# Three edge sweeps of a graph network on one core: who fetches the last column of every second group

## What is computed

```python
# layer 1 (four heads); layer 0 is alike, with one head and no edge term
alpha = a_src[src_a] + a_dst[dst_a] + a_edge
alpha = jnp.where(alpha > 0, alpha, NEG_SLOPE * alpha)
amax = jax.ops.segment_max(alpha, dst_a, num_segments=n)
alpha = jnp.exp(alpha - amax[dst_a])
denom = jax.ops.segment_sum(alpha, dst_a, num_segments=n)
out = jax.ops.segment_sum(alpha[:, :, None] * h[src_a], dst_a, num_segments=n)  # alpha over denom
# layer 3 (relations)
h = jnp.einsum('nd,rdo->rno', x, W_rel)
msg = h[edge_type, src]
agg = jax.ops.segment_sum(msg, dst, num_segments=n)
```

## Time and profile before

| | |
|---|---|
| Median of 3 runs | 9807.24 us (9797.97 to 9817.08) |
| Span of the profiled execution | 9691.9 us |
| The profiled execution's own time | not given beside its span |
| Gathers of the first attention sweep, first to last start | 324.2 to 2511.9 us |
| Gathers of the second attention sweep | 2950.7 to 6034.3 us |
| Gathers of the relation sweep | 6526.4 to 9500.0 us |
| Busy | POOL 51%, DVE 35%, ACT 11%, PE 7% |

### The profile page before, as it was taken

How to read it: one execution, slowest core, us unless ns; L and a number is a source line. 1 busy time by engine, 2 the same in 40 slices (tenths; PEclk the granted TensorE clock), 3 DMA queues, 4 the chain that set the end, 5 groups by cost and what they waited for, 6 DMA issues and landing times.

```text
span 9691.9 us, 57509 instructions
## 1 busy us (share of the span) xinstructions
PE 645.5 (7%) x2460; PEld 429.5 (4%) x2460; DVE 3381.8 (35%) x6204; ACT 1028.8 (11%) x3093; POOL 4970.1 (51%) x5237
## 2 busy tenths in 40 slices
PE   1100000000140000000000000580000000000000
PEld 1000000000140000000000000240000000000000
DVE  6555555555563222222222222761111111111113
ACT  1222222222120000000000000460000000000000
POOL 5766666666457444444444444216444444444445
PEclk7555555555565555555555555795555555555555
DMA  4456666666433222222222222452222222222222
GB/s 158 145 178 199 194 186 196 192 193 202 155 108 94 67 72 70 69 73 69 73 70 72 70 71 69 164 200 71 64 67 66 68 68 68 65 70 68 68 68 97
DMA packets 344911, 1045.34 MB, mean 108 GB/s; under 512 B 111529, under 2 KB 139564, under 8 KB 306594
## 3 DMA queue, kind: packets, MB, share of 16 engines
q1 hardware_dynamic: 157746, 670.54, 19.3%
q0 software_dynamic: 172192, 365.19, 14.8%
q10 hardware_dynamic: 14544, 5.93, 0.3%
HBM read 527.27 MB, written 513.96 MB: 107 GB/s over the span
## 4 chain that ended last, share of the span: by engine, by line
SPq 36%; issue 31%; DVE 14%; another core or an unknown queue 8%; PE 3%; POOL 3%; ACT 3%; ACTq 1%; DMA 1%; DVEq 0%; POOLq 0%
SPq L250 21%; SPq L249 7%; SPq L247 7%; DVE ps L1256 2%; DVE ps L1281 2%; POOL node_sums L1387 1%; DVE edge_rows L1286 1%; ACT edge_rows L1220 1%; DVE edge_rows L1264 1%; PE ps L2028 1%; ACTq L250 1%; DVE edge_logit L1356 1%; DVE feat_prod L1343 1%; DVE fine L592 1%
## 5 line engine op out<-in xcount | busy, mean ns | idle before, releaser
L1158 POOL DMA_INDIRECT edge_rows<-table_b,src_i x1523 | 1440.8, 946 | 1642.7 <-DMA sums_b<-edge_rows 1161.0
L2113 POOL DMA_INDIRECT edge_rows<-table_rel,rel_row x1523 | 1440.7, 946 | 1641.1 <-DMA sums_rel<-edge_rows 1096.3
L1158 POOL DMA_INDIRECT edge_rows<-table_a,src_i x1568 | 1485.0, 947 | 702.8 <-issue 487.3
L2197 DVE TENSOR_TENSOR edge_rows<-edge_rows,ps 128x1024 f32<-128x1024 f32 x195 | 237.9, 1220 | 2301.3 <-DMA edge_rows<-table_rel 2220.7
L1286 DVE TENSOR_TENSOR edge_rows<-edge_rows,ps 128x1032 f32<-128x1032 f32 (+1 forms) x390 | 484.2, 1241 | 962.5 <-remote 726.8
L1350 DVE TENSOR_TENSOR edge_rows<-edge_rows,ps 128x2112 f32<-128x2112 f32 (+1 forms) x99 | 230.9, 2332 | 1010.1 <-ACT ps L1223 961.8
L1220 ACT ACTIVATE edge_rows<-edge_rows,weight_decay 128x129 f32<-128x129 f32 x1560 | 493.6, 392 | 211.5 <-issue 211.3
L1281 DVE TENSOR_TENSOR ps<-edge_rows,ps 128x1032 f32<-128x1032 f32 (+1 forms) x390 | 485.6, 1245 | 8.6 <-issue 1.9
L1316 DVE TENSOR_TENSOR z<-edge_rows,dst_logit 128x16 f32<-128x16 f32 (+2 forms) x198 | 40.1, 203 | 1194.2 <-DMA edge_rows<-table_b 1171.4
L1223 ACT ACTIVATE ps<-weight_decay 128x128 f32<-128x128 f32 (+1 forms) x99 | 27.7, 280 | 3036.5 <-DVE weight_decay L1337 1562.8
L2144 ACT ACTIVATE ps<-keep 128x16 f32<-128x16 f32 x98 | 19.6, 201 | 2985.8 <-issue 1534.7
(11 more groups left out here) (296 smaller groups left out, 3207.3 us busy)
## 6 DMA issues: line engine op xcount, KB each, us to landing
sums_a<-edge_rows SPq DMA_DIRECT2D x98, 2064.0 KB
sums_b<-edge_rows SPq DMA_DIRECT2D x98, 1120.0 KB, 4.2
edge_rows<-in_ea SPq DMA_DIRECT2D x98, 1024.0 KB
sums_rel<-edge_rows SPq DMA_DIRECT2D x98, 1024.0 KB, 3.9
table_rel<-rel SPq DMA_DIRECT2D x98, 512.0 KB
edge_rows<-table_b SPq DMA_DIRECT2D x2880, 0.5 KB
edge_rows<-table_b ACTq DMA_DIRECT2D x2880, 0.5 KB
edge_rows<-table_rel ACTq DMA_DIRECT2D x2880, 0.5 KB
```

Of the source, the lines that this page charges most:

```text
L1158: e.indirect_dma_start(out=rows[:, s, i, 0:L.W], out_offset=None, in_=L.table, in_offset=bass.IndirectOffsetOnAxis(ap=src[:, at:at + 1], a ...
L2113: e.indirect_dma_start(out=rows[:, s, i, :], out_offset=None, in_=table_rel, in_offset=bass.IndirectOffsetOnAxis(ap=rel_row[:, at:at + 1], ...
```

## The change

The class `Helped` becomes `Gathers`, which only counts what POOL's gathers add to the semaphores. In the second attention sweep and in the relation sweep POOL gathers all sixteen columns of all 98 groups, and SP and ACT fetch nothing. `helped_src`, `helped_rel`, the two transposes and five small DVE instructions that made them in the graph stage, the registers and the extra waits of DVE go. Slots, stores, waits before the gathers and all arithmetic of the sweeps stay. The core of the diff (left out are the declarations of the two tiles and of the registers):

```diff
@@ -208,52 +205,26 @@
 
-    LAST = GC - 1
-
-    def every(n, first):
-
-        return {g: h for h, g in enumerate(range(first, NG - 1, n))}
-
-    def helped_columns(ap, place):
-
-        at = [natural(g, LAST) for g in place]
-        return ap[:, at[0]:at[-1] + 1:at[1] - at[0]]
-
-    helped_b = every(2, 7)
-
-    class Helped:
-
-
-        def __init__(self, name, place, index, table, W, rows, NS, stored, summed):
-            self.place, self.index, self.table, self.W = place, index, table, W
-            self.rows, self.NS, self.stored, self.summed = rows, NS, stored, summed
-            self.by_pool = {g: 16 * sum(GC - (i in place) for i in range(g % NS, g + 1, NS)) for g in range(NG)}
-            self.by_pool[NG - 1] -= 16 * GK
+    class Gathers:
+
+
+        def __init__(self, NS):
+            self.NS = NS
             self.first_half = sem_of("edges_first_half", 16 * GK)
-            self.fetched = [sem(f"{name}_helped{i}") for i in range(3)] if place else []
-
-        def all_by_pool(self, slot):
-            return self.by_pool[max(g for g in range(NG) if g % self.NS == slot)]
-
-        def fetch(self, e, regs, g, p0, n):
-
-            if g not in self.place:
-                return
-            h, s = self.place[g], g % self.NS
-            e.wait_ge(*self.stored[s].at(16 * (g // self.NS)))
-            e.wait_ge(*self.summed.at(g - self.NS + 2))
-            for p in range(p0, p0 + n, len(regs)):
-                m = min(len(regs), p0 + n - p)
-                e.load(regs[0:m], self.index[h:h + 1, p:p + m])
-                for i in range(m):
-                    row = e.snap(regs[i])
-                    e.dma_start(self.rows[p + i:p + i + 1, s, LAST, 0:self.W], self.table[bass.ds(row, 1), :]
-                                ).then_inc(self.fetched[h % 3].sem, 16)
+            self.slot = [sem_of(f"edges_gathered{i}", self.total(max(g for g in range(NG) if g % NS == i)))
+                         for i in range(NS)]
+
+        def total(self, g):
+            return 16 * GC * (g // self.NS + 1) - (16 * GK if g == NG - 1 else 0)
+
+        def landed(self, g, i):
+            return self.first_half if g == NG - 1 and i < GK else self.slot[g % self.NS]
+
+        def wait_half(self, e):
+            e.wait_ge(*self.first_half.at(16 * GK))
 
         def wait(self, e, g):
-            if g in self.place:
-                h = self.place[g]
-                e.wait_ge(*self.fetched[h % 3].at(16 * P * (h // 3 + 1)))
+            e.wait_ge(*self.slot[g % self.NS].at(self.total(g)))
 
@@ -470,8 +441,6 @@
         hc = sb("head_count", [P, GK])
-        helped_f = sb("helped_f", [P, 2, P])
-        helped_floated, helped_turned = sem("helped_floated"), sem("helped_turned")
         weights = Weights(A, sb, io["a_w"], io["a_att_src"], io["a_att_dst"])
@@ -638,9 +607,6 @@
                 t = then(e.tensor_copy(tmp_e[:, :], src[:, :]))
-                then(e.memset(helped_f[:, :, :], 0.0))
-                e.wait_ge(*step.at(step.n))
-                e.tensor_copy(helped_f[:, 0, 0:len(helped_b)], helped_columns(tmp_e, helped_b)).then_inc(helped_floated.sem, 1)
                 e.wait_ge(*zero_stored.at(N_ZERO))
@@ -649,7 +615,6 @@
                 then(e.tensor_copy(rel_row[:, :], tmp_e[:, :]))
-                e.tensor_copy(helped_f[:, 1, 0:len(helped_b)], helped_columns(tmp_e, helped_b)).then_inc(helped_floated.sem, 1)
                 yield
@@ -733,9 +698,6 @@
             then(e.tensor_copy(sum_row[:, :], s2[:, :]))
-            e.wait_ge(*helped_turned.at(1))
-            then(e.tensor_copy(helped_src[:, :], ps[:, 7, 0:P]))
-            then(e.tensor_copy(helped_rel[:, :], ps[:, 7, P:2 * P]))
 
@@ -743,10 +705,6 @@
                     table.t_turn(e, i)
-            e.wait_ge(*helped_floated.at(2))
-            for i in range(2):
-                done = e.transpose(ps[:, 7, i * P:(i + 1) * P], helped_f[:, i, :], ident[:, :])
-            done.then_inc(helped_turned.sem, 1)
 
@@ -1105,8 +1063,7 @@
         summed = sem_of("edges_summed", NG)
-        helped = Helped(L.name, helped_b if L.AE else {}, helped_src, L.table, L.W, rows, NS, stored, summed)
-        gathered = [sem_of(f"edges_gathered{i}", helped.all_by_pool(i)) for i in range(NS)]
+        gathers = Gathers(NS)
 
@@ -1152,13 +1109,12 @@
                     e.wait_ge(*summed.at(g - NS + 2))
-                for i in range(GC - (g in helped.place)):
+                for i in range(GC):
                     at = natural(g, i)
-                    landed = helped.first_half if g == NG - 1 and i < GK else gathered[s]
                     e.indirect_dma_start(
...
                         in_offset=bass.IndirectOffsetOnAxis(ap=src[:, at:at + 1], axis=0)
-                    ).then_inc(landed.sem, 16)
+                    ).then_inc(gathers.landed(g, i).sem, 16)
                     if g == 0 and i == GC // 2:
@@ -1193,9 +1149,6 @@
                             ).then_inc(stored[g % NS].sem, 16)
-                if L.AE:
-                    helped.fetch(e, regs_sync, g + 4, 0, P // 4)
-                    helped.fetch(e, regs_sync, g + 3, P // 4, P // 4)
             for s in range(NS):
@@ -1224,8 +1177,6 @@
                                  group_columns_of_heads(edge_logit[:, :, :], g), ACT.Copy).then_inc(terms_copied.sem, 1)
-                    helped.fetch(e, regs_scalar, g + 3, P // 2, P // 4)
-                    helped.fetch(e, regs_scalar, g + 2, 3 * P // 4, P // 4)
             crossing.scalar(e)
@@ -1309,10 +1260,9 @@
                     if g == NG - 1 and part == 0:
-                        e.wait_ge(*helped.first_half.at(16 * GK))
+                        gathers.wait_half(e)
                     else:
-                        e.wait_ge(*gathered[g % NS].at(helped.by_pool[g]))
-                        helped.wait(e, g)
+                        gathers.wait(e, g)
                     t_logit = then(e.tensor_tensor(z[:, b, ts, :, :], maxima[:, ts, :, :], logit[:, ts, :, :], ALU.add))
@@ -2091,8 +2041,7 @@
         summed = sem_of("edges_summed", NG)
-        helped = Helped("rel", helped_b, helped_rel, table_rel, D, rows, NS, stored, summed)
-        gathered = [sem_of(f"edges_gathered{i}", helped.all_by_pool(i)) for i in range(NS)]
+        gathers = Gathers(NS)
         crossing = Crossing("cross", rows[:, (NG - 1) % NS, GC - GK:GC, :], sb("border_state", [P, NV + 1])[:, :],
@@ -2143,8 +2089,6 @@
                              ).then_inc(keep_copied.sem, 1)
-                helped.fetch(e, regs_scalar, g + 2, P // 2, P // 4)
-                helped.fetch(e, regs_scalar, g + 1, 3 * P // 4, P // 4)
 
@@ -2177,7 +2121,7 @@
                         e.wait_ge(*keep_copied.at(1))
-                        e.wait_ge(*gathered[0].at(helped.by_pool[0]))
+                        gathers.wait(e, 0)
                     keep_now = bc(ps[:, 4 + g % 2, t * GK:(t + 1) * GK].unsqueeze(2), [P, GK, D])
@@ -2189,10 +2133,9 @@
                     if t == 0 and g == NG - 1:
-                        e.wait_ge(*helped.first_half.at(16 * GK))
+                        gathers.wait_half(e)
                     elif t == 0 or g == NG - 1:
-                        e.wait_ge(*gathered[s].at(helped.by_pool[g]))
-                        helped.wait(e, g)
+                        gathers.wait(e, g)
                     e.wait_ge(*step.at(done))
```

More of the change, by code:

```diff
@@ L145, in build @@
     head_row = sb_kept("head_row", [P, GK], I32)
-    helped_rel = sb_kept("helped_rel", [P, P], I32)
     sum_row = sb_kept("sum_row", [P, NJ], I32)
@@ L163, in build @@
     cut = sb_edges("cut", [P, EC])
-    helped_src = sb_edges("helped_src", [P, P], I32)
     spread = sb_edges("head_spread", [B.H + 1, B.WN])
     spread_a = sb_edges("head_spread_a", [A.H, A.WN])
-    regs_sync, regs_scalar = [], []
     stage_done = sem("stage_done")
@@ L2283, in _ @@
         def _(e):
-            regs_sync.extend(e.alloc_register(f"row_sync{i}") for i in range(32))
             graph.sync(e)
@@ L2302, in _ @@
         def _(e):
-            regs_scalar.extend(e.alloc_register(f"row_scalar{i}") for i in range(32))
             graph.scalar(e)
```

## The result

The changed kernel takes 7947.81 us (7932.74 to 7959.31, 4 runs) against 9811.34 us (9797.97 to 9817.08) for the kernel before: ratio 0.8099, 95% interval 0.8087 to 0.8111. The prediction was 7610 us with a range of 7560 to 7850. Direction and kind of gain came as forecast. A gain of 1863.5 us is 334 us less than the 2197 of the sum, and the time lies 98 us outside the range. The profiled execution has a span of 7948.2 us and an own time of 7959.31: 11.1 us lie around the span.

A forecast was written before the change was run, and what follows sets the result against it. The prediction took SP's row-by-row fetch as the bound, and POOL's gathers after the change. Gains of 1120.7 + 1012.0 + 31 + 32 + 1.2 = 2196.9 us, taken from 9807.2, gave 7610 us, range 7560 to 7850.

The forecast's parts named there:

- the sum: Whole kernel: gains of 1120.7 and 1012.0 us in two sweeps, 31 and 32 at their ends, 1.2 in the graph stage.
- What bounds the kernel: Second attention and relation sweeps: SP's fetch, 28.23 of 33.16 us between stores, sets the pace; without it POOL does.
- The rate of the gathers: Second attention and relation sweeps: 20.03 us a group on POOL for all 98 groups, gaining 1120.7 and 1012.0 us.
- a rival for one sweep with 0.11: Second attention sweep falls to the first's 22.34 us a group through VectorE or ACT: 225 + 32 us more, 7867 us; chance 0.11.
- Slow issue: Second attention sweep: instructions wait longer while POOL gathers without pause, so VectorE takes 18.90 us a group, 1.13 below POOL.
- The ends of the sweeps: After the last gather, waits of 61.99 and 42.67 us shrink to 30 and 12, gaining 32 and 31 us.
- What lies around the span: Outside the traced span of before: 115.3 us up to the median of the runs, taken as unchanged.
- The rule on spreading: Both changed sweeps: concentrating fetches on POOL would cost 56 us a sweep; rival slower than before, 9920 us, chance 0.01.
- Half the gain by late landing: Both changed sweeps: stores and gathers meet at the DMA engines, some 25 us a group, 980 us more, 8590 us; chance 0.03.

The follow-up runs named there:

- experiment 6: Kernel before; in the relation sweep POOL gathers 8 of a group's 16 columns, the others left out, SP and ACT fetch as before: 8925.71 us.
- 2: Changed kernel; in the relation sweep each gather fetches only the rows of partitions 0 to 63, the other edges left out: 7917.85 us.
- 3: Changed kernel with five small PE matmuls added for each group's sum in the relation sweep: 7987.32 us.
- 4: Changed kernel with each group of the relation sweep stored a second time, into a tensor of its own: 7889.4 us.
- 7: Changed kernel with a one-element memset on POOL ahead of each gather of the relation sweep: 7954.46 us.
- experiment 1: The kernel before, unchanged, profiled a second time: 9701.27 us, span 9696.3 us.
- 5: Kernel before with row-by-row fetching only in the second attention sweep; POOL gathers all sixteen columns in the relation sweep: 8903.8 us.
- 8: Changed kernel with two pauses of POOL in the relation sweep, twenty memsets behind group 40 and five behind group 70: 7953.05 us.
- 9: The changed kernel without further edits, timed once more against the kernel before: 7925.92 us, ratio 0.8097.
- 10: Kernel before with SP and ACT helping in every fourth group instead of every second: 8842.84 us, ratio 0.9034.
- 11: Kernel before with SP and ACT helping in every eighth group instead of every second: 8315.69 us, ratio 0.8490.

## Why the prediction was right and wrong

**What bounds the kernel: right, and incomplete.** SP's fetch set the pace of both sweeps; without it POOL does, its waits for stores are gone, and VectorE starts 1.6 us after POOL's last gather of a group has ended, as before. What I had not seen is that SP's 0.88 us a row was half POOL's doing (experiment 6).

**The rate of the gathers: the step that failed.** "98 groups x 20.03 us" took a pace read in the first groups of the relation sweep, before the first fetch. That is the stretch in which the gathers still run at their fast pace. It holds for eleven groups; then the rate is 1.40 us a gather, set neither by rows (2), PE (3), stores (4) nor other instructions of POOL (7). What does set it was not found. The term should have been 11 x 20.0 + 87 x 22.40 = 2169 us for each sweep. That is 206 us more than forecast, twice, and 411 of the 453 us of the miss between the profiled executions.

**The first attention sweep: half read.** A warning stood there. With all sixteen columns on POOL it took 22.34 us a group in the kernel before. I gave that to ACT and VectorE, because VectorE's waits at L1286 could be seen, and priced it as a rival for one sweep with 0.11. The trace of before bears this out as far as it goes. What POOL's gathers of that sweep sat idle for (us, times):

```profile
  issue: 487.3, 1531
  DVE edge_rows L1286: 215.5, 37
```

These 215.5 us are nearly all of the 229 us that the sweep takes over a pace of 20.0 us a group. What I didn't ask is when they fall. Here, too, in every trace, the first ten or eleven groups run at the fast pace (the first one of all a little longer); then groups of 26.6 us, in which POOL waits 6 to 7 us for VectorE, alternate with groups of 20.0, and the average is 22.5 to 22.7 us, just over 22.40. By POOL's rate alone the sweep would take 2169 us; it takes 2180 to 2201. So it is likely that the limit of the gathers stands behind this sweep as well, and that the slow instructions of the other engines are its other side, but no run tests that. The rival's 225 us were near the 205.5 by which the second attention sweep was off, but by a cause that was not at work in that sweep: there VectorE waits for POOL. The relation sweep, too simple for that cause, was left at 20.03.

**Slow issue: wrong size, no effect.** I took 18.90 us as VectorE's time for a group of the second attention sweep, from one group. Such groups exist, 15.8 to 19.2 us long, but only at the start of the sweep; once VectorE waits for every group it needs 9.8 on average. The margin to POOL was not 1.13 us but over 12.

**The ends of the sweeps: too cautious.** 11.8 and 7.5 us, where I took 30 and 12 and named 12 and 7.5 as the least.

**What lies around the span: wrong.** I took 115.3 us as lying around the span. It is 5 us (experiment 1: 9701.27 to 9696.3), and 11.1 in the changed kernel's profiled execution. The traced execution of before was most likely one on a chip where this kernel takes some 9700 us. On the others the stages that did not change are also longer: the first gather starts at 336 to 341 us in every trace of experiments 5 to 11 and of the changed kernel, at 316 to 328 in 1 to 4. On the chip of experiments 1 to 4 the changed kernel with two stores, its sweeps as long as without them, has a span of 7879.0 us, 69 us less than the 7948.2 above. This can account for the +64.8 us; where every part of them lies stays open. The wrong base made the forecast's own number look better, and that was luck: against the traced execution it missed by 453 us, against the medians by 338.

**The rule on spreading.** The rivals weighed a rule by which the work should be spread over queues. More help was slower in each of three steps (experiments 9 to 11). The Trainium skill, Perfetto Trace Analysis, section DMA Optimizations, says that spreading over engines may help where descriptor generation is the bottleneck; the runs here speak against it for single rows on SP and ACT, with 64 DMAs on each helper for one of POOL's. POOL is the bottleneck now, and taking 12 columns a sweep off it costs 390 us.

**Half the gain by late landing:** out, VectorE starts 1.6 us after POOL's last gather.

## What to carry to other kernels

Read a pace late in a long loop, not in its first iterations: eleven groups of 98 at full speed are enough to mislead a forecast by a tenth. Where a loop of the same kind already runs without the thing to be removed, its rate is the first candidate for the new rate. A visible wait does not settle that it has a cause of its own: look also at when the wait begins. An engine that takes small pieces off a bottleneck has to be counted together with what the two do to each other: here the 128 single-row DMAs of a column cost 16 to 23 us to spare POOL 1.40.

## What the runs showed of the hardware

- Indirect gathers on POOL, one after the other, start every 1.25 us for about 180 and every 1.40 us from there on. A pause refills what was used up: 16.7 us for about 4 groups, 43.6 us for 11. Rows (64 or 128), other data traffic (71 to 142 GB/s), small matmuls on PE and small instructions between the gathers leave the 1.40 us as it is. What it is made of was not found.
- With a memset between the gathers the fast stretch was two groups long instead of eleven, at the same steady rate. Open.
- While gathers go on, DMA instructions on SP take longer: 0.42 us a row without them, 0.56, 0.88, 1.96 and 3.58 us as POOL's pauses get fewer. On PE a matmul of 0.17 us starts every 2.8 us then, and again every 0.21 us from some 20 us after the last gather on.
- Chips differ: the kernel before takes 9671 to 9701 us on one and 9790 to 9811 on others. Its second attention sweep takes 3083 us on the first and 3107 to 3111 on another (experiments 5 and 6, which leave that sweep as it was), while the steady 22.40 us of the gathers was the same on all.
